# Later slots for the weights of groups 1 to 3 in the ramp of a fused cross-attention and FFN kernel

## The reference, cut to what matters

```
q = _ln(_fp8_linear(ln_out, wq));  k = _ln(_fp8_linear(ln_out, wk));  v = _fp8_linear(ln_out, wv)
core = _gqa(q, k, v)
qx = _ln(_fp8_linear(ln_out, wqx));  kx, vx = split(cond @ w_kv_x.T);  kx = _ln(kx)
xout = _gqa(qx, kx, vx)
x = x + tanh(g_xattn) * (quant(concat(core, xout)) @ wproj.T) * scale
x = x + tanh(g_ffn) * ffn(_layernorm(x))     # ternary weights, 8-bit activations
```

## Time and profile before

| | us |
|---|---|
| median of 3 runs | 1812.07 (1807.82 to 1817.33) |
| the profiled execution | 1815.84 |
| its span | 1814.1 |
| mean granted clock of TensorE | 0.976 |

### The profile page before, as it was taken

One profiled execution on the slowest core, in us unless ns is written; L12 is line 12 of the kernel. 1 busy time (PEld: TensorE's weight loads), 2 busy tenths in 40 slices (PEclk: granted clock), 3 DMA queues, 4 the chain that ended last, 5 costly groups with the idle time before them and its releaser, 6 DMA issues.

```text
span 1814.1 us, 35237 instructions
## 1 busy us (share of the span) xinstructions
PE 1620.1 (89%) x11164; PEld 1005.9 (55%) x11164; DVE 1533.6 (85%) x3391; ACT 1371.8 (76%) x3439; POOL 1100.2 (61%) x1421
## 2 busy tenths in 40 slices
PE   2368899889999999999999898999999978999997
PEld 1345555555666665666566555666666633444443
DVE  7568889999897899989887999999988876777776
ACT  6458999879989998999998788899988872222222
POOL 3677888877887777787776666777767641000000
PEclk9689999999999999999999999999999999999999
DMA  3257888779999998999897989999998896243200
GB/s 104 90 151 164 186 194 190 178 169 230 230 244 196 218 226 191 205 217 250 193 216 169 224 192 200 222 229 225 251 222 169 184 246 216 70 112 87 76 24 18
DMA packets 669596, 325.48 MB, mean 179 GB/s; under 512 B 552288, under 2 KB 595424, under 8 KB 669152
## 3 DMA queue, kind: packets, MB, share of 16 engines
q1 hardware_dynamic: 669408, 323.17, 79.2%
HBM read 140.61 MB, written 48.23 MB: 104 GB/s over the span
## 4 chain that ended last, share of the span: by engine, by line
PE 45%; DVE 24%; ACT 12%; issue 8%; POOL 7%; DMA 4%; SPq 0%; ACTq 0%; POOLq 0%; DVEq 0%
PE psum L699 8%; PE psum L654 8%; PE psum L687 7%; PE psum L742 6%; PE psum L717 6%; DVE pp L987 5%; DVE nmx L977 5%; PE psum L661 3%; PE psum L760 3%; ACT pp L1334 2%; DMA pt<-pp 2%; ACT psum L1323 2%; PE psum L674 2%; ACT raw L1254 2%; DVE xh L960 1%
## 5 line engine op out<-in xcount | busy, mean ns | idle before, releaser
L687 PE MATMUL psum<-qk 128*128 128x512 f16 x1536 | 422.5, 384 | 21.6 <-DVE pp L987 15.8
L699 PE MATMUL psum<-pt,vv 128*128 128x512 f16 x1536 | 399.3, 383 | 37.2 <-ACT cy L1342 22.4
L654 PE MATMUL psum<-wbt,xqt 128*128 128x256 f16 (+1 forms) x4096 | 408.7, 249 | 22.1 <-DVE xqt L904 11.4
L1323 ACT ACTIVATE psum<-psum,nmx 128x512 f32<-128x512 f32 x512 | 352.4, 688 | 69.6 <-DVE nmx L977 68.0
L654 PEld LDWEIGHTS psum<-wbt,xqt 128*128 128x128 f16 x4096 | 329.5, 99 | 136.2 <-issue 18.4
L987 DVE SCALAR_TENSOR_TENSOR pp<-psum,prs,pp 128x512 f16<-128x512 f32 x512 | 378.7, 740 | 3.3 <-ACT pp L1334 3.3
L1334 ACT ACTIVATE pp<-psum,prs 128x512 f16<-128x512 f32 x512 | 366.0, 715 | 6.2 <-DMA pt<-pp 5.9
L977 DVE TENSOR_REDUCE nmx<-psum 128x1 f32<-128x512 f32 x512 | 344.8, 674 | 28.6 <-PE psum L687 28.0
L699 PEld LDWEIGHTS psum<-pt,vv 128*128 128x128 f16 x1536 | 147.5, 98 | 234.5 <-issue 54.2
L1579 POOL TENSOR_TENSOR qk<-y,qk 128x512 f16<-128x512 f32 x192 | 231.8, 1207 | 16.0
L687 PEld LDWEIGHTS psum<-qk 128*128 128x128 f16 x1536 | 143.8, 99 | 105.4 <-DVE pp L987 24.8
(11 more groups left out here) (176 smaller groups left out, 2792.3 us busy)
## 6 DMA issues: line engine op xcount, KB each, us to landing
wbt<-ws SPq DMA_DIRECT2D x192, 256.0 KB, 3.7
ws<-wbt SPq DMA_DIRECT2D x64, 256.0 KB, 4.1
catd<-cy SPq DMA_DIRECT2D x64, 256.0 KB, 3.2
raw<-in_wgu SPq DMA_DIRECT2D x64, 256.0 KB, 3.6
raw<-in_w SPq DMA_DIRECT2D x32, 384.0 KB, 3.9
wbt<-catd SPq DMA_DIRECT2D x6, 2048.0 KB, 9.8
pt<-pp SPq DMA_TRANSPOSE x512, 3.8
raw<-in_wp SPq DMA_DIRECT2D x32, 256.0 KB, 3.6
```

Of the source, the lines that this page charges most:

```text
L654: ins = e.matmul(bank[:, o0:o0 + c1 - c0], xv[:, v, kt * 512 + tt * 128:kt * 512 + (tt + 1) * 128], wb[i][:, h, kt, c0:c1], start=kt == 0 ...
L687: ins = e.matmul(SB(n), qk[i][:, jq, u, ss], qk[i][:, jk, w, :], start=k == 0, stop=k == 2)
L699: ins = e.matmul(OB, v[:, t, u, att, :], src[:, w, t, :], start=t == 0 and k == 0, stop=t == 3 and k == 2)
L1323: e.activation(SB(n), SB(n), ACT.Exp, bias=nmx[:, k], accum_out=psm[:, k]).then_inc(s["exp"], 1)
```

## The change

The slots of the loads of groups 1 to 3 come from a table of their own; groups 4 to 7 keep theirs. In group 1, tile 3 goes from slot -20 to -16, tiles 4 and 5 from -20 and -19 to -14 and -13. In group 2, tiles 4, 5, 0, 1, 2, 3 go from -13, -12, -8, -4, -3, -1 to -8, -7, -4, 0, 1, 2. In group 3, tiles 4, 5, 0 go from 3, 4, 8 to 5, 6, 9; the others stay at 12, 13, 15. All steps that count from the load move with it. The group factors, the stores and the projections stay.

```diff
-RAMP_LOAD = (-27, -26, -25, -20, -20, -19)
+RAMP_LOAD = (-27, -26, -25, -16, -14, -13)
+FIRST_LOADS = {1: RAMP_LOAD, 2: (-4, 0, 1, 2, -8, -7), 3: (9, 12, 13, 15, 5, 6)}
@@
 def load_slot(it, t):
 
-    return RAMP_LOAD[t] if it == 1 else (it - 2) * SLOTS + TILE_LOAD[t]
+    return FIRST_LOADS[it][t] if it in FIRST_LOADS else (it - 2) * SLOTS + TILE_LOAD[t]
```

## The result

The changed kernel is slower: 1824.52 us median (1819.07 to 1833.07, 16 runs) against 1814.08 (1807.56 to 1817.33, 16 runs), a ratio of 1.006, 95% interval 1.0048 to 1.0073, or about 10 us: slower by 0.6%, clear of 1. Forecast were 7 us more, 1819, within 1804 to 1826. Its profiled span is 1826.2 us against 1814.1. Lines of the changed kernel stand one lower than before: L863 is the old L862.

The account below looks back on a forecast made before the run. ScalarE was taken to bound the steady state at about 3 us a slot, with no engine full in the ramp. Terms -8.7, +8.7, -2, +6 and +2.9 gave about +7 us on the median 1812.07: 1819, range 1804 to 1826.

Parts of the forecast that it names:

- What bounds the kernel: Steady state: ScalarE is full at about 3 us a slot, so time won or lost before stays in the end time.
- Part 1: Ramp up to slot -7: later group 1 loads free PE, tile 1.0 comes 8.7 us ahead, bounds 5 to 11.
- Part 2: Slots -7 to -4: load (2,5) waits for the split of (1,4), delaying spread, split and PE; 8.7 us given back.
- Part 3: Slots -4 to 6: lighter GpSimd weight work, sums of group 2 waiting 0 to 1 us each; 2 us ahead.
- Part 4: Slots 6 to 11: late last split of group 2 and late kv factor hold PE; 6 us lost, 4 behind.
- GpSimd's queue from tile 1.3's rstd on ... 12.4 us without a gap: Before group 2's projection: GpSimd's queue ends at 144.8, so PE starts group 2 3.5 us later than before.
- Part 5: Slots 12 to 16: loads of (3,1), (3,2) wait for later kv splits of group 3, stalling VectorE; 2.9 us lost.
- The sum: Whole kernel: -8.7 and +8.7 in the ramp, -2 by slot 6, +6 to slot 11, +2.9 to 16; about +7 us.
- The kept lead: Rival, chance 0.2: slots -7 to -4 give back only 2 to 4 us of the ramp's lead; 1807 or 1803.
- The cancelling case: Rival, chance 0.18: the losses of slots 6 to 16 overlap, VectorE waiting once; 0 to +3 us, 1813.
- slower by more: Rival, chance 0.12: transposes behind loads (3,1), (3,2) land last, delaying ScalarE in slots 15, 16 and cooling PE; +12, 1824.
- The signs: Expected in the new trace: two PE waits of 6 to 9 us, tile 1.0's statistics near 92 and 104, named load waits.

Follow-up runs that it names:

- e3: The changed kernel with a fourth raw buffer, so each load waits for one split fewer; ratio 1.0004 to the kernel before.
- e4: The kernel before with the same fourth raw buffer and no slots moved; ratio 0.9963 to the kernel before.
- e10: The kernel before with four raw buffers and the kv tiles of group 1 one slot later; ratio 0.9955 to the kernel before.
- e9: The changed kernel with buffers of their own for the two kv tiles of group 3 only; ratio 1.0035 to the kernel before.
- e1: The changed kernel with group 1 back in its old slots, groups 2 and 3 still late; ratio 1.0062 to the kernel before.
- e8: e3 with tiles 1, 2, 3 of group 2 two, two and one slots earlier; ratio 0.9978 to the kernel before.
- e5: The changed kernel's idea with about half the shift and three raw buffers; ratio 1.003 to the kernel before.

## Why the prediction was right, point by point

- **What bounds the kernel.** Held as far as it was compared. From slot 16 to the last slot compared, 56, the changed kernel runs 10.9 us behind (10.6 to 11.1): no slot wins any of it back, and e3, e4, e10 keep their place the same way. e9 is an exception, it loses 1.9 us more behind slot 16.
- **Part 1, 8.7 us ahead at tile 1.0.** Held: 11.2 by the clock of the span, 10.1 with the 1.1 of start-up taken off, within the bounds of 5 to 11. One step inside it was off: PE had its parts before the spread done at 69.7, not at about 76, so it paused 13.3 us and not some 8. The spread came at 82.58 instead of 84.3 all the same, since it waits for DVE and not for PE. Part 3 of tile 0.3 behind the pause was priced 2.75 and took 2.20 at a granted clock of 0.55, and part 3 of tile 1.0 took 2.74 after its wait of 8.3 us.
- **Part 2, all of it given back.** The mechanism held: 3.37 us of wait for (2,5), then spread, split, part 3 of tile 1.0 at 98.89. From the end of the split of (1,4) to that part it took 5.8 us where 6.0 were forecast, only all of it some 2.4 us earlier. So statistics B came 2.1 us earlier instead of 0.3 later, and 9.1 us of the lead were given back, not quite all. e1 shows that this part and part 1 together bring nothing, or less. The load of (2,5), issued at 93.08, had landed when DVE began at 96.03, 2.95 us later, near the 3.0 of the sum. The 2.6 us that the prediction works out from the Trainium skill (DMA: Bandwidth & Descriptors, Anatomy of one DMA) rest on a formula that the page fits to DMAs issued by GpSimd. These are issued by SyncE, and the measured 3.0 decides.
- **Part 3, 2 us ahead at slot 6.** Measured 3.6, both at the row maximum of slot 6 and at the statistics of tile 1.3; 2.5 with the start-up taken off. The three sums of group 2 waited 0.77, 0.29 and 0.83 us, as forecast (0 to 1).
- **Part 4, 6 us lost between slots 6 and 11.** This term was too small: from slot 6 to 11 it is 11.0 us (-3.6, from the same timelines as the table, to 7.4). The step that failed is "GpSimd's queue from tile 1.3's rstd on ... 12.4 us without a gap": it has a gap. From 130.78 to 147.12 it takes 16.3 us, the 12.4 of work and 3.92 of waiting for DVE. I had checked the releases of (2,5), (2,1) to (2,3) and (3,1), (3,2), but not of (3,4) and (3,5), which wait for the splits of (2,1) and (2,2), moved from slots 2 and 3 to 6 and 7 while the sums moved only from 5 and 6 to 7 and 8. That is DVE's 3.40 + 3.66 us and POOL's 3.92 in front of the spread. e9 takes just this out, and then the part comes as forecast: POOL's row of work runs without a gap from 130.99 to 143.37, 12.4 us, and the row maxima of slots 10 and 11 start at 147.12 and 152.76, forecast 147.4 and 153, against 150.87 and 156.43 in the changed kernel. From slot 6 to 11 e9 loses 7.1 us, 3.9 less than the changed kernel; the 1.1 us above the forecast 6 are its larger lead at slot 6 (3.4 instead of 2). How the 3.9 us divide between DVE's sums and SP's transposing DMAs isn't shown, since e9 frees both. The rest, the last split against PE and the factor in front of the head transpose (1.62 us of wait), held; e3 and e8 show the first, with the wait for it at 8.2 and 3.6.
- **Part 5, 2.9 us.** Measured 3.5 (7.4 at slot 11 to 10.9 at 16). Of the two waits, forecast at 2 to 4 us each, the first is within (2.73 us) and the second below (0.71); the transposes behind the loads may hold the rest, which wasn't tried alone.
- **The sum.** +7 forecast, +10.9 at slot 16 and about +10 timed. The missing 3 to 4 us are the 5.0 that part 4 lacked and 0.6 of part 5, less 1.6 us of lead at slot 6 that was larger than forecast. That the lead made up for a third of the left-out term is luck. Of the 5.5 us between the forecast 1819 and the measured 1824.52, 2.0 are the kernel before itself, whose median was 1812.07 when the forecast was made and 1814.08 here; the measured median lies 1.5 us below the upper end of the range.
- **The rivals.** The kept lead falls by the trace: 9.1 us go between statistics A and B of tile 1.0. Its own sum was also off, as it counts the 2 us of part 3 twice; the 6.9 us of later cost have them taken off already. The cancelling case falls too: the kernel loses 11.0 us from slot 6 to 11 and another 3.5 to slot 16, one on top of the other. The rival "slower by more" gave nearly the measured time, 1824, but by another mechanism than the one that was found.
- **The signs.** PE's wait of 15.1 us became one of 13.3, not one of 6 to 9; the second, 8.3, is in its range. DVE's 3.37 us for the last kv tile of group 2 and PE's wait for a split before group 2 came as stated. Statistics A and B of tile 1.0 came at 89.81 and 101.66, each some 2 us earlier than said.

## What to carry to other kernels

Work that is moved later keeps its buffers longer: with a ring of three, each load's release moves with the split three places before it, so for every tile write down slot of release, slot of load and slot of use, also for the groups that weren't meant to change. One slot from release to use was never enough here: 3.37, 3.40 and 3.66 us of wait for the three kv tiles (landing 3.0), 2.73 and 0.71 for two weight tiles. The same 15 us hole that invited the later slots was better met by one more buffer, lent from a tile not yet in use: 0.9963 against 1.006, with nothing moved.

A wait that goes isn't time won. In e9 DVE's 7.1 us of waiting went and 3.7 came off the path, in e5 the named waits went and the kernel was still slower; the start of the same instruction in both traces, slot by slot, showed what was left.

## What the runs showed that I had not expected

The pace behind the disturbance is repeated closely: in the changed kernel 38 of the 41 row maxima of slots 16 to 56 start between 10.8 and 10.9 us after those of the kernel before. Start-up differs more than that: in the kernels with three shared buffers (e9 among them) the statistics of tile 0.1 lie between 1.9 us before and 0.2 after those of the kernel before. With four buffers they lie 2.2 to 3.0 us before; whether that is start-up or the buffer wasn't separated. Nor can a lead be cleared of start-up by plain subtraction: the changed kernel and e9 hold the same loads up to slot 4 and stand at -4.5 and -4.7 at slot 0, though at tile 0.1 they lie 1.3 us apart.
